# Upper and lower products of a split-precision attention kernel: the lower ones lag one group behind

## What is computed

```python
Wh = X @ W.T
s_i = Wh @ r_src
s_j = Wh @ r_dst
e = s_i[:, None] + s_j[None, :]
e = jnp.where(e >= 0, e, ALPHA * e)
e = jnp.where(A == 0, -jnp.inf, e)
attention = jax.nn.softmax(e, axis=1)
output = attention @ Wh
x = _layernorm(x + jax.nn.gelu(output, approximate=False), axis=-1)
```

## Time and profile before

| | us |
|---|---|
| median of 3 runs | 1563.2 (1562.9 to 1565.87) |
| the profiled execution | 1564.42 |
| its span, first to last instruction | 1562.7 |
| TensorE busy | 1542.8 |
| VectorE busy | 1484.2 |
| ScalarE busy | 1211.6 |
| GpSimd busy | 460.8 |

### The profile page before, as it was taken

The page is one execution under the profiler, slowest core; times in us unless marked ns, Lnnn a source line. Parts: engine busy times, 40 slices in busy tenths (PEclk is TensorE's granted clock), DMA queues, the critical chain, the costliest instruction groups (busy, mean ns, idle before and its releaser), DMA issues.

```text
span 1562.7 us, 37408 instructions
## 1 busy us (share of the span) xinstructions
PE 1542.8 (99%) x12839; PEld 1538.1 (98%) x12839; DVE 1484.2 (95%) x1857; ACT 1211.6 (78%) x1609; POOL 460.8 (29%) x667
## 2 busy tenths in 40 slices
PE   9999999999999999999999999999999999999996
PEld 8999999999999999999999999999999999999996
DVE  5899999999999999999999999999999999999996
ACT  6878888877787777787787777878778777777774
POOL 1112223333323333322333332233332233323222
PEclk9999999999999999999999999999999999999998
DMA  9746778769588686858877776877778687787861
GB/s 201 131 62 89 107 94 117 106 81 133 73 119 118 101 111 90 121 75 126 115 106 101 101 115 80 128 104 103 109 102 117 83 128 96 99 121 93 115 88 42
DMA packets 295102, 163.99 MB, mean 105 GB/s; under 512 B 12320, under 2 KB 291104, under 8 KB 295072
## 3 DMA queue, kind: packets, MB, share of 16 engines
q0 software_dynamic: 278976, 142.12, 69.5%
q1 hardware_dynamic: 15472, 21.28, 5.1%
q10 hardware_dynamic: 624, 0.26, 0.1%
HBM read 289.41 MB, written 8.42 MB: 191 GB/s over the span
## 4 chain that ended last, share of the span: by engine, by line
PE 95%; issue 3%; ACT 1%; POOL 1%; DMA 0%; DVE 0%; POOLq 0%; ACTq 0%; DVEq 0%; SPq 0%
PE acc L815 30%; PE acc L825 30%; PE acc L818 30%; PE acc L722 1%; PE acc L736 1%; PE acc L747 1%; PE acc L742 1%; ACT P_hi L477 0%; DMA w_in<-in_L_gnn_W 0%; ACT gates L381 0%; POOL fits L339 0%; POOL adj_in L273 0%; POOL fits L341 0%; PE acc L781 0%; PE acc L754 0%
## 5 line engine op out<-in xcount | busy, mean ns | idle before, releaser
L815 PE MATMUL acc<-WV_hi,P_hi 128*128 (+1 forms) x4096 | 998.4, 282 | 4.1 <-ACT P_hi L477 3.6
L818 PE MATMUL acc<-WV_lo,P_hi 128*128 (+1 forms) x4096 | 996.8, 281 | 0.0
L815 PEld LDWEIGHTS acc<-WV_hi,P_hi 128*128 128x128 f32 x4096 | 773.7, 189 | 6.2 <-ACT P_hi L477 4.1
L818 PEld LDWEIGHTS acc<-WV_lo,P_hi 128*128 128x128 f32 x4096 | 771.7, 188 | 0.0
L477 ACT CAST P_hi<-Pw 128x1024 fp32r<-128x1024 f32 x512 | 535.9, 1047 | 287.9 <-DVE Pw L613 152.5
L613 DVE SCALAR_TENSOR_TENSOR Pw<-R_row,X,gatesT 128x512 f32<-128x512 f32 x1024 | 710.8, 747 | 0.5 <-issue 0.5
L623 DVE TENSOR_TENSOR P_lo<-Pw,P_hi 128x1024 fp32r<-128x1024 f32 x512 | 625.5, 1222 | 40.2 <-ACT P_hi L477 35.9
L273 POOL DMA_DIRECT2D adj_in<-in_adj x512 | 330.4, 654 | 886.2 <-ACT gates L381 856.6
L825 PE MATMUL acc<-WV_hi,P_lo 128*128 (+1 forms) x4096 | 575.4, 283 | 0.0
L381 ACT ACTIVATE gates<-adj_in 128x1024 uint8<-128x1024 bf16 x512 | 536.8, 1048 | 29.1 <-DMA adj_in<-in_adj 28.9
L825 PEld LDWEIGHTS acc<-WV_hi,P_lo 128*128 128x128 f32 x4096 | 526.6, 189 | 0.0
(11 more groups left out here) (102 smaller groups left out, 345.0 us busy)
## 6 DMA issues: line engine op xcount, KB each, us to landing
adj_in<-in_adj POOLq DMA_DIRECT2D x512, 256.0 KB, 5.4
out<-y SPq DMA_DIRECT2D x64, 128.0 KB, 6.1
y<-in_x POOLq DMA_DIRECT2D x60, 128.0 KB, 5.9
Pw<-in_x SPq DMA_DIRECT2D x46, 128.0 KB, 5.5
R_row<-w_rows SPq DMA_DIRECT2D x15, 256.0 KB, 6.7
x_res<-in_x SPq DMA_DIRECT2D x20, 128.0 KB, 5.2
w_in<-in_L_gnn_W SPq DMA_DIRECT2D x1, 256.0 KB, 4.4
Pw<-in_x ACTq DMA_DIRECT2D x2, 128.0 KB, 4.1
```

What stands on the lines that cost most here:

```text
L815: nc.tensor.matmul(acc[r_][:, v, 0:HC], P_hi[:, u % 2, par, bass.ts(v, P)], WV_hi[:, k, :], start=(first and u == 0 and par == 0), stop=False)
L818: nc.tensor.matmul(acc[r_][:, v, 0:FOUT], P_hi[:, u % 2, par, bass.ts(v, P)], WV_lo[:, k, :], start=False, stop=False)
```

## The change

TensorE's queue is written in another order. After the 16 upper products of a group come the 8 lower products of the group *before* it, not of the group itself; the lower products of the last group of a row block come at the end of the block, after those of the last but one. The count of products, their operands and the accumulator stay the same. The last upper product of each group now signals a new semaphore `s_used` (it also starts at 2), and ScalarE's cast of group G waits for `s_used >= G + 1` and `s_lo >= G - 1` in place of `s_free >= G + 1`. `s_free` is signalled by the last lower product as before, and VectorE's wait for it (in `low_part`) is left as it was.

```diff
+        s_used = sem("upper_weights_used")
...
-                            act.wait_ge(s_free, G + 1)
+                            act.wait_ge(s_used, G + 1)
+                            if not (not before and c == 0 and u < 2):
+                                act.wait_ge(s_lo, G - 1)
...
             pe.sem_inc(s_free, 2)
+            pe.sem_inc(s_used, 2)
...
+                def lower_products(ah, r_, c, u, final=False):
+                    G = GB * (2 * ah + r_) + GP * c + u
+
+                    pe.wait_ge(s_lo, G + 1)
+                    for par in range(2):
+                        k = CP * c + 2 * u + par
+                        for v in range(RT):
+                            last = nc.tensor.matmul(acc[r_][:, v, 0:HC], P_lo[:, u % 2, par, bass.ts(v, P)],
+                                                    WV_hi[:, k, :], start=False, stop=(final and par == 1))
+                    last.then_inc(s_free, 1)
...
-                                nc.tensor.matmul(acc[r_][:, v, 0:FOUT], P_hi[:, u % 2, par, bass.ts(v, P)],
-                                                 WV_lo[:, k, :], start=False, stop=False)
-
-                        pe.wait_ge(s_lo, G + 1)
-                        for par in range(2):
-                            k = CP * c + 2 * u + par
-                            for v in range(RT):
-                                last = nc.tensor.matmul(acc[r_][:, v, 0:HC], P_lo[:, u % 2, par, bass.ts(v, P)],
-                                                        WV_hi[:, k, :], start=False,
-                                                        stop=(final and u == GP - 1 and par == 1))
-                        last.then_inc(s_free, 1)
+                                last = nc.tensor.matmul(acc[r_][:, v, 0:FOUT], P_hi[:, u % 2, par, bass.ts(v, P)],
+                                                        WV_lo[:, k, :], start=False, stop=False)
+                        last.then_inc(s_used, 1)
+                        if u > 0:
+                            lower_products(ah, r_, c, u - 1)
+                        elif not first:
+                            lower_products(ah, r_, c - 1, GP - 1)
+                        if final and u == GP - 1:
+                            lower_products(ah, r_, c, u, final=True)
```

## The result

The changed kernel takes 1714.0 us (median of 4 runs, 1711.2 to 1715.6) where the kernel before takes 1563.7 (median of 4): a ratio of 1.0957, 95% interval 1.0942 to 1.0973. The forecast was 1699 with a range of 1678 to 1717. The profiled execution took 1715.63 us with a span of 1713.9.

The account below looks back on a forecast made before the run. TensorE's own pace was taken as the bound, with at most about 6 us to win. Piece borders 131.0, row-block borders 3.0 and table loads 4.1, less 2.7 of removed waits, gave 135.4 us more: 1699 us, range 1678 to 1717.

Parts of the forecast that it names:

- The chain that closes at each border: From a piece's last group to the next's first: 3.93 us against 2.864 of work, 1.17 lost at 112 borders, 131.0 us.
- Release: Border chain's first step: from the start of the last group's upper products to VectorE's subtraction, 0.26 us.
- subtraction: Border chain's second step on VectorE: the last group's subtraction up to the start of the next weights, 1.14 us.
- weights: Border chain's third step: VectorE's weights for the new piece's first group up to ScalarE's cast, 1.45 us.
- the cast up to the first product: Border chain's last step: ScalarE's cast to TensorE's first product, 1.08 us, with 1.19 as the alternative bound.
- Borders of row blocks: Between row blocks: 3.82 us of work against a 3.93 us chain, 0.2 us lost 15 times, 3.0 us.
- Table loads: In 7 row blocks ScalarE's gelu table load delays a piece's second group, 3.79 us after the first: 4.1 us more.
- The costs put at nothing: Product order's pace, address instructions, signal `s_used` and the cast's added wait for `s_lo`: each cost 0.
- Rival 1: At piece borders the subtraction finds its buffer free, so the casts' head start wins: faster, 1557 us; chance 0.03.
- Rival 2: ScalarE's cast of the second group is also late by 0.3 us at 112 borders: 34 us more, 1732; chance 0.05.
- Rival 3: Recurring waits at borders make the clock fall for 3 us each: 146 us more, 1845 us; chance 0.04.
- Rival 4: The change does nothing, since TensorE was hardly waiting and VectorE catches up: 1563 us; chance 0.02.

Follow-up runs that it names:

- the best kernel: Kernel before with the cast released by the upper products and a new piece's first weights ahead of the old piece's last lower weights: 1559.1 us, ratio 0.9969.
- Experiment 1: Changed kernel with VectorE making the weights of a new piece's first group ahead of the lower weights of the old piece's last group: 1562.9 us.
- experiment 2: Changed kernel with VectorE's transpose moved behind the subtraction of a piece's last group, ahead of the next piece's first weights: 1959.4 us.
- (3): Changed kernel with a third buffer of lower weights for a piece's last group, the last row block's residual load left out to make room: 1641.5 us.
- (5): Each part of the change alone on the kernel before: the cast's earlier release with the old order of products 1560.7 us, the lagging lower products 2306.1 us.
- the lag alone: Changed kernel with the cast waiting for `s_free` as before, so only the lower products' one-group lag remains against the kernel before: 2306.1 us.
- experiment 4: Changed kernel with TensorE's loop over the six middle pieces written out: 1748.0 us, ratio to the kernel before 1.1194.

## Why the prediction was right, point by point

- **The bound and the ceiling of the gain.** TensorE's pace was the bound and about 6 us were to be had: the best kernel gets 0.31%, 5 us, and its 12288 products take 1466.8 us at a pace that allows 1466. Shown.
- **The chain that closes at each border.** Right in place, order and count. Release 0.26 forecast, 0.27 measured; subtraction 1.14 and 1.14; weights 1.45 and 1.44. Shown by taking it apart (1), lengthening it (2) and letting its subtraction start earlier (3). The idle time came to 119.8 us where I had said about 100.
- **The mis-sized term: from the cast to the first product.** The step "the cast up to the first product, 1.08 us" was too short; it measured 1.19 at 96 of 112 borders, 0.11 us more at each, some 11 us in all, most of the 15 us by which the forecast was low. The earlier trace rows had the right value, and I used it as a bound only. The difference wasn't chance: both waits of the earlier trace rows fell on products whose addresses are constants, the one of the earlier trace rows on a product in the loop, where the queue has an address instruction that carries the wait ahead of the matmul. The question to ask was in which of the two parts the borders lie.
- **Borders of row blocks.** 4.5 us in place of 3.0, 0.20 of wait and 0.10 of restart each; small. The chain is 4.04 us there in the median, in place of 3.93: the step from the weights to the cast takes 1.52 us at a row block's start, in place of 1.45.
- **Table loads.** 3.1 us in place of 4.1. The second group came 3.66 us behind the first (496.65 to 500.31) in place of 3.79, as the first now bears the longer step itself.
- **The costs put at nothing.** The second wait of the cast didn't end last (483.8 of the cast's 485.5 us of idle time are put down to `Pw`), nor did the new signal cost: with it and the old order the kernel got faster (5).
- **Rival 1, the borders don't close.** False for this kernel, as the queue showed. Experiment 1 makes its condition true and took 1562.9 us, not this rival's 1557: there the casts' head start is small (1.39 us from cast to product at a border), and the 7 waits behind table loads grew.
- **Rival 2, ScalarE late as well.** False: at no border but the 7 with a table load did the second group wait.
- **Rival 3, the clock.** False here: outside the prologue and the tail no stretch at 0.50. It came true in experiment 2. The Trainium skill (TensorE: Matmul & The Clock Gate, A second HAM failure mode: psum-queue depth-cycling) has the clock go back and forth if short idle times between groups are frequent. The runs agree with it in one case and not in two: recurring waits of 1.2 us (this kernel) and of 1.45 us, 495 of them (the lag alone, 5), left the clock at 1.00; waits of 2.6 us once in 14 us went with a fall at 40 of 127 borders (2). The measurement decides, and in these runs it was the longer waits and not the more frequent ones that went with the fall; with the seven waits of 4.5 to 5.8 us in experiment 4 it fell every time. Experiment 2 and the second part of 5 are one execution each.
- **Rival 4, nothing changes.** False: 1714.0 us.

## What to carry to other kernels

When a consumer is moved back in one engine's queue, the buffer that it gives back comes later by as much; look at every engine that waits for that buffer, and then at what stands *behind* that wait in its queue. An engine with 3% of slack can take a wait where the next engine has a head start and not where it has none: here three of four groups took it. Behind the subtraction of the fourth stand the weights of the very next group, with nothing made ahead, and it cost 9% of the run. Moving one step in the queue cured it; one buffer more cured half.

## What the runs showed of the hardware that I had not expected

- A wait that sits on an address instruction ahead of a matmul costs 0.096 us more than one that sits on the matmul: 1.194 against 1.098 us from the cast's start to the product, at 96 and 16 borders of the changed kernel, and at 112 of 112 the shorter one once the loop was written out.
- Writing out a loop on TensorE cost more than it saved: about 4.9 us with no releaser at each jump back over the longer body, with 16 KB transfers of kind "instruction" in each of these idle times, and a fall of the clock with it (products 0.21 us apart instead of 0.12 in the 3 us shown).
- The restart after a wait cost 0.10 us behind the first product (0.22 us to the second) at full clock, behind waits of 0.2 us (row blocks), 1.2 us (pieces), 1.45 us (the lag alone) and 2.6 us (experiment 2) alike.
